# A two-layer graph kernel: layer 2's probabilities turned by the transposing DMA, and a new order of all engines where layer 1 meets layer 2

## The reference

```python
# layer 1 (12 heads of 64)
h = feat_in @ W;  th = tanh(h)
attn = softmax(mask(leaky_relu(th @ w_src + (th @ w_dst).T)))     # per graph, 64 x 64
feat_out = elu(attn @ h + b)
gate = sigmoid(feat_in @ H_w.T + H_b)
x = layernorm(x + gate * feat_out + (1 - gate) * x)
# layer 2 (6 heads of 128)
q, k, v = x @ Wq + bq, x @ Wk + bk, x @ Wv + bv
probs = softmax(q @ k.T / sqrt(128) + where(adj, 0, -9e15))       # per graph, 64 x 64
x = layernorm(x + (probs @ v) @ Wf + bf)
```

## Time and the profile before

| | us |
|---|---|
| median of 3 runs | 2766.53 (2765.67 to 2773.51) |
| the profiled execution, its own time | 2766.33 |
| its span, first to last instruction | 2764.6 |
| mean granted TensorE clock | 0.997 of full speed |
| PE busy | 2726.9 |
| DVE busy | 1668.8 |
| ACT busy | 1160.3 |
| POOL busy | 1066.3 |

### The profile page before, as it was taken

How to read it: one execution, slowest core, us unless ns; L and a number is a source line. 1 busy time by engine, 2 the same in 40 slices (tenths; PEclk the granted TensorE clock), 3 DMA queues, 4 the chain that set the end, 5 groups by cost and what they waited for, 6 DMA issues and landing times.

```text
span 2764.6 us, 51821 instructions
## 1 busy us (share of the span) xinstructions
PE 2726.9 (99%) x20988; PEld 2517.8 (91%) x20988; DVE 1668.8 (60%) x3334; ACT 1160.3 (42%) x3045; POOL 1066.3 (39%) x630
## 2 busy tenths in 40 slices
PE   8999999999999989999999999999999999999998
PEld 6877778888788889999999999999999999999998
DVE  6888998888888754444454444454445445444443
ACT  5666776666666633322332233322332233223322
POOL 2453344433444134433444343434443343434340
PEclk9999999999999999999999999999999999999999
DMA  5656665555555512222213222222222222222220
GB/s 180 173 131 145 164 160 145 139 139 139 141 137 143 175 59 69 69 71 81 70 58 81 76 75 58 79 72 71 69 68 71 81 70 58 81 81 70 58 70 23
DMA packets 306894, 269.49 MB, mean 97 GB/s; under 512 B 227808, under 2 KB 244192, under 8 KB 306656
## 3 DMA queue, kind: packets, MB, share of 16 engines
q1 hardware_dynamic: 306656, 266.19, 35.5%
HBM read 142.65 MB, written 75.89 MB: 79 GB/s over the span
## 4 chain that ended last, share of the span: by engine, by line
PE 85%; DVE 5%; DMA 4%; issue 2%; POOL 2%; ACT 2%; SPq 1%; DVEq 0%; ACTq 0%; POOLq 0%
PE ps_hg L1036 21%; PE ps_a L1199 14%; PE ps_k L70 14%; PE ps_q L70 14%; PE ps_a L70 14%; PE ps_c L1165 2%; PE ps_s L1140 2%; PE ps_pv L1068 1%; DMA dst_all<-dst_scratch 1%; ACT logits L564 1%; PE ps_t L1055 1%; PE ps_pt L1165 1%; DMA dst_scratch<-dst 1%; PE ps_pt L1147 1%; DVE logits L770 1%
## 5 line engine op out<-in xcount | busy, mean ns | idle before, releaser
L1036 PE MATMUL ps_hg<-w_hi,xT 128*128 128x512 f32 x2268 | 745.6, 401 | 8.3 <-DVE h_one L803 8.2
L1036 PEld LDWEIGHTS ps_hg<-w_hi,xT 128*128 128x128 f32 x2268 | 426.1, 188 | 112.6 <-issue 11.3
L1036 PE MATMUL ps_hg<-w_lo,xT 128*128 128x512 f32 x1134 | 448.4, 395 | 0.0
L70 PE MATMUL ps_k<-x1T_hi,wk_hi 128*128 128x256 f32 x1152 | 329.1, 286 | 0.0
L70 PE MATMUL ps_q<-x1T_hi,wq_hi 128*128 128x256 f32 x1152 | 323.5, 281 | 1.4 <-DVE x1T_lo L910 1.4
L70 PE MATMUL ps_q<-x1T_lo,wq_hi 128*128 128x256 f32 x1152 | 322.6, 280 | 0.0
L70 PE MATMUL ps_k<-x1T_lo,wk_hi 128*128 128x256 f32 x1152 | 321.9, 279 | 0.0
L70 PE MATMUL ps_q<-x1T_hi,wq_lo 128*128 128x256 f32 x1152 | 321.9, 279 | 0.0
L70 PE MATMUL ps_k<-x1T_hi,wk_lo 128*128 128x256 f32 x1152 | 321.1, 279 | 0.0
L496 POOL TENSOR_TENSOR th_src<-th,wsrc_all 128x768 f32<-128x768 f32 x64 | 118.3, 1848 | 483.7 <-DVE dst_all L783 463.4
L648 ACT ACTIVATE qT<-ps_q,bq_col 128x256 f32<-128x256 f32 x192 | 80.5, 470 | 479.3 <-PE ps_q L70 479.3
(11 more groups left out here) (144 smaller groups left out, 5814.2 us busy)
## 6 DMA issues: line engine op xcount, KB each, us to landing
x_tok<-x SPq DMA_DIRECT2D x64, 384.0 KB, 4.1
dst_all<-dst_scratch SPq DMA_DIRECT2D x128, 192.0 KB, 3.4
gate_scratch<-gate SPq DMA_DIRECT2D x64, 384.0 KB, 2.6
feat_scratch<-feat SPq DMA_DIRECT2D x128, 192.0 KB, 2.8
feat_in<-feat_scratch SPq DMA_DIRECT2D x62, 384.0 KB, 3.1
gate_in<-gate_scratch SPq DMA_DIRECT2D x62, 384.0 KB, 3.7
x_even<-x SPq DMA_DIRECT2D x16, 768.0 KB, 4.2
x_odd<-x SPq DMA_DIRECT2D x16, 768.0 KB, 4.4
```

The costliest lines, as they stand in the source:

```text
L70: ins = pe.matmul(out, left[a][c], right[b][c], start=(n == 0), stop=(n == len(terms) - 1))
L1036: ins = pe.matmul(ps_hg[:, cols], left[a][c], right[b][c], start=(c == 0 and n == 0), stop=(c == KC - 1 and n == 2))
```

## The change

1. **Probabilities of groups 2 to 31.** No PE transpose. POOL splits `scores_sb` into planes of 16-bit halves (`split_p1`), SP issues a transposing DMA of 4 blocks (`turn_p1`), and `join_block` writes the halves into `probs1T`: ACT for the first tile and, of pair 2, for both; DVE for the second tile of pairs 0 and 1. The planes lie in the last two blocks of `cT_lo`. `probs_out(G, 1)` comes after `exps(G, 2)` on ACT and after `logits_of(G, 2)` on DVE.
2. **The gate.** ACT makes `0.5 tanh + 0.5` (`whole_gate`) and POOL's addition goes; `mix` multiplies x by 2 and EPS is no longer scaled.
3. **The edge.** Tile 63 of layer 1 leaves its `src_scores`, `elu(61)` and `store_feat(61)` to after the first transposes of layer 2. PE starts these without waiting for the weights; `first_query` waits for Wq alone and goes chunk by chunk as x1 arrives. SP loads the first feat and gate before the last weights and x of group 1 right after PE's last transposes of layer 1; the leftovers of ACT and DVE (weight chunks, `elu`, `attention`) are spread anew.
4. **DVE's order in a group**: `mix`, `input_moments` and `rstd_start` ahead of `logits_of(G, 2)`, `rstd_end` ahead of `normalise(G, 2)`.

```diff
+        def join_block(copy, buf, t, g, signal):
+            s = graph(g)
+            out_ = probs1T[s, buf, :, s].bitcast(U16).rearrange("p (h t) (n l) -> p l h t n", t=GT, l=2)[:, :, :, t, :]
+            copy(out_, planes_p1T[t * NODES:(t + 1) * NODES, :, :, s]).then_inc(signal, 1)
+
+        def pair_of(G, j):
+
+            return PAIRS * (G - BY_DMA) + j + 1
...
-                if T >= 2:
+                if 2 <= T < NT - 1:
                     store_feat(T - 2)
...
-            sp.wait_ge(g_done, NT)
-            for n in range(EARLY_W1, 4 * KC):
-                load_chunk(sp, w1_chunks[n], w1_in[n])
-            store_gate(NT - 1)
-            store_feat(NT - 2)
-
...
+            sp.wait_ge(g_done, NT)
             sp.wait_ge(src_done, NT)
             sp.wait_ge(z_done, NT)
             feat_and_gate(1, 0)
+            for n in range(EARLY_W1, 4 * KC):
+                load_chunk(sp, w1_chunks[n], w1_in[n])
+            store_feat(NT - 3)
             sp.wait_ge(pt_done, NT)
             sp.dma_start(x1_tok[1][:, :, :], x_g[1]).then_inc(x1_in[1], 16)
+            store_gate(NT - 1)
+            sp.wait_ge(mixed, GT + 1)
+            feat_and_gate(1, 1)
+            store_feat(NT - 2)
             store_feat(NT - 1)
             sp.wait_ge(gate_stored, 16 * NT)
             sp.dma_start(bf_all[:, :], bf.partition_broadcast(P)).then_inc(bf_in, 16)
-            sp.wait_ge(mixed, GT + 1)
-            feat_and_gate(1, 1)
...
+            def turn_p1(G, j):
+                sp.wait_ge(split_p1_done, pair_of(G, j))
+                for joined_ in (block0_done, block1_done):
+                    sp.wait_ge(joined_, 2 * (PAIRS * G + j))
+                sp.dma_start_transpose(planes_p1T.rearrange("p l h n -> p (l h) n"),
+                                       planes_p1.rearrange("p l (h m) -> p (l h) m", h=2)).then_inc(turned_p1, 16)
...
+                if BY_DMA <= G + 1 < NG:
+                    for j in range(PAIRS):
+                        turn_p1(G + 1, j)
...
-                pool.tensor_scalar(gate_, gate_, 1.0, None, ALU.add).then_inc(gate_ready, 1)
...
+            def split_p1(G, j):
+                pool.wait_ge(probs_done, PAIRS * G + j + 1)
+                if pair_of(G, j) > 1:
+                    pool.wait_ge(turned_p1, 16 * (pair_of(G, j) - 1))
+                pool.tensor_copy(planes_p1[:, :, :], scores_sb.rearrange("p k m -> p (k m)").bitcast(U16)
+                                 .rearrange("p (d l) -> p l d", l=2)).then_inc(split_p1_done, 1)
...
-                if 1 <= G < NG - 1:
-                    for t in range(GT):
+                for t in range(GT):
+                    if 1 <= G < NG - 1:
                         feat_less_x(G + 1, t, feat_in[:, :])
                         times_gate(G + 1, t, feat_in[:, :], gate_in[:, :])
+                    if G >= BY_DMA:
+                        split_p1(G, t)
+                if G >= BY_DMA:
+                    split_p1(G, GT)
...
+            def whole_gate(G, t, gate_):
+                if G == 0:
+                    act.wait_ge(fg_first[t], 32)
+                else:
+                    act.wait_ge(fg_in, 32 * (GT * (G - 1) + t + 1))
+                act.activation(gate_, gate_, ACT.Copy, scale=0.5, bias=0.5).then_inc(gate_ready, 1)
...
             def probs_out(G, j):
-                act.wait_ge(pt1_done, PAIRS * G + j + 1)
-                for g in range(2):
-                    copy_block(act.copy, (G + j) % 2, 0, g, ptc_act)
+                if G < BY_DMA:
+                    act.wait_ge(pt1_done, PAIRS * G + j + 1)
+                    for g in range(2):
+                        copy_block(act.copy, (G + j) % 2, 0, g, block0_done)
+                else:
+                    act.wait_ge(turned_p1, 16 * pair_of(G, j))
+                    for g in range(2):
+                        join_block(act.copy, (G + j) % 2, 0, g, block0_done)
+                    if j == PAIRS - 1:
+                        for g in range(2):
+                            join_block(act.copy, (G + j) % 2, 1, g, block1_done)
...
             round_x1(0)
+            for n in range(EARLY_W1 - LATE_W1, EARLY_W1):
+                w1_round(act, n)
+            leaky_scores(NT - 1)
             copy_probs(NT - 2)
-            leaky_scores(NT - 1)
-            gate_of(NT - 1)
             act.wait_ge(cols_in, 48)
             act.wait_ge(thsrc_done, NT)
             q_out(0, 0)
             bias_of_mask(0)
             exp_scores(NT - 1)
+            k_out(0, 0)
+            copy_probs(NT - 1)
             for n in range(3):
-                w1_round(act, EARLY_W1 + n)
-            k_out(0, 0)
-            elu_exp(NT - 2)
-            copy_probs(NT - 1)
-            for n in range(3, KC):
                 w1_round(act, EARLY_W1 + n)
...
+                    if G + 1 < NG:
+                        whole_gate(G + 1, 0, gate_in[:, :])
                 q_out(G, 1)
+                if G == 0:
+                    whole_gate(1, 0, gate_in[:, :])
                 exps(G, 0)
+                if G == 0:
+                    gate_of(NT - 1)
                 k_out(G, 1)
+                if G == 0:
+                    elu_exp(NT - 2)
+                    for n in range(3, KC):
+                        w1_round(act, EARLY_W1 + n)
                 q_out(G, 2)
-                if G == 0:
-                    elu_exp(NT - 1)
+                if 1 <= G < NG - 1:
+                    whole_gate(G + 1, 1, gate_in[:, :])
+                if G == 0:
                     act.wait_ge(bd_zero, 1)
                 probs_out(G, 0)
                 exps(G, 1)
                 if G == 0:
+                    whole_gate(1, 1, gate_in[:, :])
+                k_out(G, 2)
+                if G == 0:
+                    elu_exp(NT - 1)
                     for n in range(KC, KC + 3):
                         w1_round(act, EARLY_W1 + n)
-                k_out(G, 2)
                 if G == 0:
                     act.wait_ge(pv_done, NT)
                 value_out(G, 0)
-                probs_out(G, 1)
+                if G < BY_DMA:
+                    probs_out(G, 1)
                 exps(G, 2)
+                if G >= BY_DMA:
+                    probs_out(G, 1)
                 value_out(G, 1)
                 value_out(G, 2)
...
             def mix(G, t, feat_):
...
-                dve.scalar_tensor_tensor(out=x_, in0=x_, scalar=4.0, in1=feat_, op0=ALU.mult,
+                dve.scalar_tensor_tensor(out=x_, in0=x_, scalar=2.0, in1=feat_, op0=ALU.mult,
...
+                if T == NT - 1:
+                    bias_g(T)
+                    break
...
+                elif G < BY_DMA:
+                    dve.wait_ge(pt1_done, PAIRS * G + j)
                 else:
-                    dve.wait_ge(pt1_done, PAIRS * G + j)
+                    dve.wait_ge(split_p1_done, pair_of(G, j - 1))
...
             rest_x1(0)
+            src_scores(NT - 1)
+            for n in range(EARLY_W1 - LATE_W1, EARLY_W1):
+                w1_rest(dve, n)
+            elu(NT - 3)
             softmax_scores(NT - 1)
             attention(NT - 2)
             for n in range(3):
                 w1_rest(dve, EARLY_W1 + n)
-            elu(NT - 2)
-            for n in range(3, KC):
-                w1_rest(dve, EARLY_W1 + n)
-            attention(NT - 1)
 
             for G in range(NG):
                 logits_of(G, 0)
                 normalise(G, 0)
-                if G == 0:
-                    elu(NT - 1)
-                elif G + 1 < NG:
+                if G + 1 < NG:
                     mix(G + 1, 0, feat_in[:, :])
                 if G == 0:
+                    elu(NT - 2)
+                    attention(NT - 1)
+                    for n in range(3, KC):
+                        w1_rest(dve, EARLY_W1 + n)
                     dve.wait_ge(bd_zero, 1)
                 probs_out(G, 0)
                 logits_of(G, 1)
                 normalise(G, 1)
-                if G == 0:
-                    mix(1, 0, feat_in[:, :])
+                if G + 1 < NG:
+                    mix(G + 1, 1, feat_in[:, :])
+                    input_moments(G + 1)
+                    if G >= BY_DMA:
+                        rstd_start(in_newton, G + 1, EPS)
+                if G < BY_DMA:
+                    probs_out(G, 1)
+                logits_of(G, 2)
+                if G >= BY_DMA:
+                    probs_out(G, 1)
+                else:
+                    rstd_start(in_newton, G + 1, EPS)
+                if BY_DMA <= G < NG - 1:
+                    rstd_end(in_newton, G + 1)
+                normalise(G, 2)
+                if G == 0:
+                    elu(NT - 1)
                     for n in range(KC, KC + 3):
                         w1_rest(dve, EARLY_W1 + n)
-                elif G + 1 < NG:
-                    mix(G + 1, 1, feat_in[:, :])
-                    input_moments(G + 1)
-                probs_out(G, 1)
-                logits_of(G, 2)
-                if 1 <= G < NG - 1:
```

(73 more changed lines are left out.)

7 lines of the change are left out of this document (5 added, 2 removed).

## The result

| | before | after |
|---|---|---|
| median, us | 2769.59 (14 runs, 2765.67 to 2775.96) | 2776.18 (14 runs, 2767.75 to 2779.20) |
| profiled execution, its own time | 2766.33 | 2773.01 |
| its span | 2764.6 | 2771.3 |

The ratio is 1.0022, 95% interval 1.0014 to 1.0030: no faster, where 2740 us was forecast. By the bound of 0.3% the kernel is the same, but all of the interval lies above 1.

A forecast was written before the change was run, and what follows sets the result against it. PE, busy 2726.9 of 2764.6 us, was taken to bound the kernel. Steady groups 18.0 plus edge 8.2, with no stall, made 26.2 us off the profiled 2766.3: 2740 us forecast, range 2730 to 2754.

The forecast's parts named there:

- PE's part in a steady group: Layer 2 groups: removing PE's transposes of the probabilities saves 0.60 us a group, 18.0 us over thirty, bounds 13.8 and 22.8.
- Whether the new way is in time: Split, turn and joins in each group: pair 2 joined by about 40.3 us, needed at 41.9, slack 1.6 us.
- Split: POOL's split of a pair's probabilities into 16-bit halves: 0.8 us, between 0.55 and 1.65.
- Landing: Transposing DMA of 4 blocks, issue to landing: 2.6 us, midway between 1.3 and 4.0, upper end 5.7.
- rival 1: The turn is late: landing near 5 us, pair after pair, 39 us more, 2779 us; chance 0.10.
- Rival 2: Part of the slack is gone: late loads or long splits cost 3 to 15 us, about 2749 us; chance 0.15.
- Join on ACT: ACT's join of 256 halves: 0.36 us each; pair 2, with all four on ACT, 1.46 us.
- Join on DVE: DVE's join of 256 halves: 0.42 us each, taken from a 256-element operation; a pair 0.85 us.
- put at 0: PE's stall in steady groups: none, with slack of 1.6 us for pair 2's joins and 2.4 before `first_context`.
- What else is added: Side costs on ACT, POOL, SP and DVE: none reach PE; `whole_gate`'s 0.85 us a tile on ACT is covered.
- The edge: Between layers 1 and 2: x of group 1 lands earlier and PE idles less, 8.2 us saved, bounds 3 and 13.
- rival 3: The edge gives nothing, because DVE, held by `mix(1, 0)`, delays leftovers PE needs: 2748 us; chance 0.10.

The follow-up runs named there:

- e6: Changed kernel with pair 1's logits and exponentials before pair 0's joins, DVE joins as reductions, pair 0's turn before feat and gate loads: 2748.30 us, ratio 0.9939.
- e7: e6 with pair 2's four joins halved between ACT and DVE instead of all on ACT: 2742.72 us, ratio 0.9915 to the kernel before.
- e3: Changed kernel with DVE's joins made as a reduction over one element instead of a copy: 2747.40 us, ratio 0.9928 to the kernel before.
- e4: Changed kernel with pair 0's turn issued ahead of the next group's feat and gate loads: 2749.14 us, ratio 0.9932 to the kernel before.
- e5: Changed kernel with POOL's `feat - x` and product each made in four quarters of 192 columns: 2759.70 us, ratio 0.9977 to the kernel before.
- e10: e7 with plain copies as DVE's joins instead of the reduction: 2789.62 us, ratio 1.0078 to the kernel before.
- e1: Changed kernel with PE's transposes of the probabilities kept in all groups; new edge, gate and DVE order stay: 2760.07 us, ratio 0.9975 to the kernel before.
- e9: Changed kernel, own order kept, with DVE's joins as a reduction and pair 2's joins halved between ACT and DVE: 2740.37 us, ratio 0.9903 to the kernel before.

## Why the prediction was wrong

**PE's part in a steady group: right.** Forecast 0.60 us, bounds 0.46 and 0.76. Measured 56.07 - 55.41 = 0.66; over thirty groups it would be 19.8 instead of 18.0.

**Whether the new way is in time: wrong, and this made the result.** By its terms:
- Split: 0.8 forecast; 0.61 when nothing is beside it, mean 1.13. Inside the bounds, but 82 of the 90 splits are held in their turn, by DVE: those that start 0.14 us behind `mix` take 1.27 us and end 0.47 after it.
- Landing: 2.6 forecast, 2.4 measured for pairs 1 and 2. Pair 0, behind feat and gate, mostly 3.7 to 5.7 after its issue, but issued 19.0 us after the group's start, so it landed at 23.4. Right. The three pairs' landings were never all near 4.6, so rival 1 is not what happened. Rival 2 had late loads of x in it, which did matter, but priced the lost slack at 0.1 to 0.5 us a group.
- Join on ACT: 0.36 forecast, 0.482 measured. Pair 2's four take 2.0 us instead of 1.46. This ate the slack of the last contexts, 0.30 us a group (1.72 to 2.02), and e6 against e7 shows the halving to be worth 5.6 us.
- **Join on DVE, "I take the 0.42 of a 256-element operation": the step that failed.** It is 0.32 alone, and 1.41 to 2.00 when it starts beside a POOL instruction. I took the price from an operation that reads PSUM and asked of POOL only whether it was busy with its own work, not whether its instructions hold DVE. In pair 0 both copies together took 3.46 instead of 0.85. Logits(1) came at 26.9 instead of 23.9, and the stall that I "put at 0" was about 1.13 us a group in the mean (the table's after less its e7: 0.46 for `kT`, 0.29 for `v_tok`, 0.30 in the contexts, 0.10 in the output, less 0.02 elsewhere), 33 us over 29 groups. The 0.30 in the contexts goes with ACT's four joins of pair 2 (e7). The waits for `kT` and `v_tok` fall from 17.8 us to 2.1 in e3, where only the form of DVE's joins changed.

The rows to see it were there before the change. In the earlier trace rows, POOL's instruction at 1544.86 ends at 1546.69, and the normalisation at 1546.33, an operation of 0.42 us, takes 0.65 and ends 0.29 after it. Here is that line over the whole kernel before (ns, min/median/max):

```profile
L931 DVE TENSOR_TENSOR scores_sb<-scores_sb,row_inv x96: 424/426/1987, 966.7 to 2733.7; 128x256 f32<-128x256 f32 x96
```

It reads two operands in SBUF. From 1010 us on, the 56 that start beside a POOL instruction average 0.635 us, the 37 others 0.424. The old joins, L264, which read PSUM, take 0.29 a copy both in the 30 pairs that overlap a POOL instruction and in the 63 that don't. The change moved DVE's joins from the second kind of operation to the first. So e3, e4, e5 and e10 have one explanation: another form, another time, a shorter neighbour, and a longer stay beside one.

The traces also show how long the hold lasts. In the kernel after, four kinds of instruction on DVE that start behind one of POOL end 0.17 (the copy), 0.28 (the normalisation), 0.81 (`mix`) and 0.81 us (a weight remainder) after it. Free, they take 0.32, 0.42, 0.95 and 0.95 us. The difference is 0.14 each time, and it is 0.14 too for POOL's split behind DVE's `mix` (0.61 free, ends 0.47 after). So, by these times, a held instruction does its work after the other has ended and none of it before; sharing in proportion would not give one constant.

The Trainium skill has the rule, on a page that I didn't weigh (SBUF — State Buffer, Who interferes with whom): VectorE and GpSimd share a pair of ports, a copy in the 2-port mode or an instruction with two SBUF inputs contends for it, whoever issues first keeps it for the whole instruction, and on trn2 `tensor_reduce` never contends. The runs agree where they touch it: copy and normalisation wait for the whole of POOL's instruction, the split for the whole of DVE's, and the reduction stays at 0.44 to 0.46. That the ports are the cause, and that this copy is in the 2-port mode, is from the page and not shown; the runs show the wait, its end and its dependence on the form.

**What else is added: right.** `whole_gate` and the rest cost nothing, by e1. **The Trainium skill's 1309 ns** for a 128x128 block (VectorE: DVE Perf Modes, The three transpose paths), which the prediction weighed, is not the price of each further block here: 4 blocks land after 2.4 us.

**The edge: right within its bounds.** Forecast 8.2, measured 6.9 (1015.73 to 1008.85). Some of this is luck: in the trace after, layer 1's last product starts 2.3 us earlier (933.44 against 935.73), and in the other traces of changed kernels it starts anywhere from 932.3 to 935.8. From it to group 1 it is 80.0 us before and 75.4 after, 73.6 to 77.6 in the others. So the edge itself gave 4.6 us, with a scatter of some 2 us either way, and there is only one trace of before. Two waits that I named have other sizes: that for the first value block's weights is 4.9 us instead of 2.3, that for `x_odd` 0.7 instead of 2; another, 2.5 for Wf, I had set against the contexts. The timeline of DVE and POOL, and then of PE, in the kernel after:

```profile
963.12 0.96 DVE L906 SCALAR_TENSOR_TENSOR x_odd<-x_odd,feat_in 128x768 f32<-128x768 f32 x1 [7.42 <-POOL feat_in L505]
...
967.04 4.29 DVE L313 TENSOR_TENSOR wv_lo<-wv_raw,wv_hi 128x768 fp32r<-128x768 f32 x3
...
968.46 2.05 POOL L500 TENSOR_TENSOR feat_in<-feat_in,x_odd 128x768 f32<-128x768 f32 x1 [5.38 <-DMA gate_in<-gate_scratch]
```
```profile
971.47 0.66 PE L70 MATMUL ps_a<-wv_hi,x1T_hi 128*128 128x384 f32 x1 [4.93 <-DVE wv_lo L313]
988.92 0.66 PE L1180 MATMUL ps_q<-ident,x_odd 128*128 128x128 f32 x4 [0.68 <-DVE x_odd L921]
994.68 0.44 PE L1289 MATMUL ps_a<-wf_hi,cT_hi 128*128 128x384 f32 x1 [2.45 <-DVE wf_lo L313]
```

DVE stands 7.4 us at `mix(1, 0)` with the remainders of Wv behind it. The mechanism of rival 3 was there but took back only part of the gain. The hold is at work here too: a remainder takes 0.95 us, but the third starts at 968.77 beside POOL's L500 and lasts 2.56, to 971.33, and PE starts at 971.47. The last remainder of Wf (992.07, again 2.56 us, beside POOL's L562) does the same to the wait of 2.45. Each of the two waits is up to 1.6 us longer for it. Four transposes take 0.66 us at 988.92, as forecast for the clock there, but it was not 1.00 all through the edge: 0.93 from 940 to 1010, against 0.90 before.

**The arithmetic afterwards.** Group 1 at 56.07 us and 29 groups of 55.41 are 1663.0, 21.1 less than before's 1684.0 (1.9 of it is what four groups of the kernel before took above 56.07); 35.4 came in on top (1698.4); the time up to group 1 gave 6.9 and the tail 0.75. Sum: 6.7 slower. Of the 35.4, e7 has 1.9 left (1664.8). e9, two edits from the kernel after, comes to 2740.37 us, the forecast: 18.1 us from the groups, 8.6 up to group 1, 0.7 from the tail. That it meets it so closely is in part luck, since 2.3 of the 8.6 lie ahead of the edge.

**Open**: why some loads of x come late. Their issue waits for a store and comes 4.1 to 4.7 us after the issue ahead of it instead of 2.4, twice in the kernel before and four times after. The kernel after has no slack for it: these four groups (12, 17, 22, 27) and one with 3.1 hold half of its loss, 17.9 of the 35.4 us. The same four groups have the late issue in e3, e6, e7 and e9 too, where the joins aren't held, and there they are 0.1 to 2.5 us above 55.41 instead of 3.4 to 4.6. So most of what a late load costs comes by way of the hold; no run took the late loads away.

## What to carry to other kernels

When work moves from PSUM to SBUF, ask of each instruction on DVE which POOL instruction runs beside it, and read the maximum of its line beside the median: a line with 0.42 us in the median and 1.99 at most has a neighbour that holds it. If DVE's copy is on a chain, give it a form that isn't held, even a slower one (0.45 us for 0.31), or put it where POOL is idle; look anew after each move, since e10's copy met another POOL instruction and lost 45 us. And price an engine's small copies by operand type and size from a row: ACT's 16-bit joins of 256 elements took 0.48 us, not something between its rows for 128 and 256 float32.

## What the runs showed of the hardware

- DVE's u16 copy from SBUF to SBUF, 64x256: 0.31 us, and up to 2.0 beside POOL, ending 0.17 us after POOL's instruction. The reduction form: 0.44 to 0.46 in every place.
- Copy, normalisation, `mix` and remainder on DVE behind an instruction of POOL, and POOL's split behind DVE's `mix`: each ends its own free length less 0.14 us after the one that holds it. The copies from PSUM (L264, 0.29) are not held.
- The transposing DMA of 4 blocks between SBUF tiles lands 2.4 us after its issue, that of 12 blocks 4.0: some 1.6 us fixed and 0.2 a block, worked out from the two. Its issue holds SP for 1.19 us.
